# A pair's context parts in an attention kernel: turned by one transpose, scaled and added by VectorE

## The reference, cut to what matters

```python
q = (x @ Wq + bq).reshape(B, S, 16, 32).transpose(0, 2, 1, 3)      # B = 2, S = 2048
k = (x @ Wk + bk).reshape(B, S, 16, 32).transpose(0, 2, 1, 3)
v = (x @ Wv + bv).reshape(B, S, 16, 32).transpose(0, 2, 1, 3)
scores = einsum('bhqd,bhkd->bhqk', q / sqrt(32), k) + attention_bias
scores = where(mask, -inf, scores)
probs = softmax(scores, axis=-1)
ctx = einsum('bhqk,bhkd->bhqd', probs, v)
```

## Time and profile before

| | |
|---|---|
| median of 3 runs | 3609.03 us (3608.39 to 3610.77) |
| span of the profiled execution | 3605.5 us; the median of the runs is 3.5 us above it |
| TensorE busy, weight loads | 98%, 68% |
| VectorE, ScalarE, POOL busy | 59%, 61%, 61% over the span |
| DMA | 828.6 MB, 230 GB/s over the span, 337 GB/s from 550 to 2350 us |
| granted TensorE clock | 0.994 of full, 1.00 from 550 to 2350 us |

### The profile page before, as it was taken

The page is one execution under the profiler, slowest core; times in us unless marked ns, Lnnn a source line. Parts: engine busy times, 40 slices in busy tenths (PEclk is TensorE's granted clock), DMA queues, the critical chain, the costliest instruction groups (busy, mean ns, idle before and its releaser), DMA issues. The chain is left out here.

```text
span 3605.5 us, 79854 instructions
## 1 busy us (share of the span) xinstructions
PE 3541.5 (98%) x32051; PEld 2435.2 (68%) x32051; DVE 2119.2 (59%) x4375; ACT 2204.3 (61%) x3175; POOL 2186.5 (61%) x782
## 2 busy tenths in 40 slices
PE   7999999999999999999999999999999999999998
PEld 3444458888888888888888888887544444444444
DVE  7676668878788787878787887876211111111102
ACT  2343369999999999999999999997210211111110
POOL 1111169999999999999999999996310110110100
PEclk9999999999999999999999999999999999999998
DMA  5555598888998888998888988887310110111002
GB/s 195 199 187 193 187 386 324 323 334 324 349 379 323 326 324 329 389 341 327 327 324 335 383 334 327 331 326 262 120 35 0 35 35 19 40 47 44 15 24 94
DMA packets 210118, 828.62 MB, mean 230 GB/s; under 512 B 25044, under 2 KB 58964, under 8 KB 134488
## 3 DMA queue, kind: packets, MB, share of 16 engines
q1 hardware_dynamic: 204532, 815.09, 59.8%
q10 hardware_dynamic: 5220, 8.42, 0.6%
HBM read 732.19 MB, written 91.23 MB: 228 GB/s over the span
## 5 line engine op out<-in xcount | busy, mean ns | idle before, releaser
L1196 POOL TENSOR_TENSOR at_tiles<-at_tiles,at_negmask 128x1920 f32<-128x1920 f32 x509 | 1951.0, 3881 | 57.8 <-DMA at_tiles<-in_bias 46.5
L1297 ACT ACTIVATE at_tiles<-at_tiles,at_rmin 128x2048 f32<-128x2048 f32 x512 | 1030.3, 2012 | 2.4 <-DVE at_rmin L1357 2.4
L1236 PE MATMUL at_ps_p<-consts,at_tiles 128*128 128x128 f32 x8192 | 1024.9, 272 | 1.9 <-ACT at_prob_t L1307 1.5
L1307 ACT ACTIVATE at_prob_t<-at_ps_p 128x512 f32<-128x512 f32 x1664 | 898.4, 603 | 153.2 <-PE at_ps_p L1236 152.3
L1236 PEld LDWEIGHTS at_ps_p<-consts,at_tiles 128*128 128x128 f32 x8192 | 939.2, 142 | 71.8 <-ACT at_prob_t L1307 1.8
L1357 DVE CUSTOM_DVE_ANT_0 at_tiles<-at_ps_s,at_tiles,at_rmin 128x1024 f32<-128x1024 f32 x512 | 657.0, 1283 | 227.1 <-PE at_ps_s L1221 226.1
L1215 PE MATMUL at_ps_s<-at_k_stack,at_q_stack 128*128 128x512 f32 x2048 | 702.0, 439 | 8.1 <-DVE at_rmin L1357 6.1
L1357 DVE CUSTOM_DVE_ANT_0 at_tiles<-at_ps_s,at_tiles 128x1024 f32<-128x1024 f32 x512 | 624.3, 1219 | 24.1 <-POOL at_tiles L1196 22.0
L1255 PE MATMUL at_ps_c<-at_prob_t,at_v 128*32 128x128 f32 x16384 | 500.3, 274 | 0.9 <-ACT at_prob_t L1307 0.9
L1255 PEld LDWEIGHTS at_ps_c<-at_prob_t,at_v 128*32 128x32 f32 x16384 | 431.6, 110 | 43.7 <-issue 42.7
L1737 PE MATMUL ff_ps_m<-ff_w,ff_hid 128*128 128x512 f32 x1024 | 441.8, 593 | 0.0
(11 more groups left out here) (193 smaller groups left out, 2631.1 us busy)
## 6 DMA issues: line engine op xcount, KB each, us to landing
at_tiles<-in_bias SPq DMA_DIRECT2D x512, 1024.0 KB, 6.2
at_k_stack<-k_hi SPq DMA_DIRECT2D x128, 256.0 KB, 5.5
at_k_stack<-k_lo SPq DMA_DIRECT2D x128, 256.0 KB, 5.4
negm<-em_mask_out SPq DMA_DIRECT2D x32, 512.0 KB, 6.6
at_q_stack<-q_hi SPq DMA_DIRECT2D x128, 128.0 KB, 5.1
at_q_stack<-q_lo SPq DMA_DIRECT2D x128, 128.0 KB, 5.2
at_v<-v SPq DMA_DIRECT2D x64, 256.0 KB, 8.1
at_negmask<-negm SPq DMA_DIRECT2D x32, 512.0 KB, 9.6
```

The costliest lines, as they stand in the source:

```text
L1196: pool.tensor_tensor(tiles[s][:, 0:PCOLS], tiles[s][:, 0:PCOLS], negm[s][:, 0:PCOLS], ALU.add).then_inc(s_pool, 1)
L1236: last = pe.transpose(ps_p[k][:, y * P:(y + 1) * P], tiles[s][:, t * P:(t + 1) * P], ident)
L1297: act.activation(tiles[s][:, :], tiles[s][:, :], ACT.Exp, bias=rmin[:, s, 1:2], scale=-1.0, accum_out=rsum[:, s:s + 1]).then_inc(s_exp, 1)
L1307: act.activation(p_t[pr % 2][:, j, 4 * c:4 * c + 4, :].rearrange("p t q -> p (t q)"), ps_p[k][:], ACT.Copy).then_inc(s_pe[k], 1)
```

## The change

`parts_sum` becomes `parts_rows`: in place of the matmul with the stacked identities stands a transpose of `cx_sb` with the ordinary identity, 128x128, into columns 128 to 255 of the same bank. It turns the parts but doesn't add the halves. `context` on VectorE then has three operations in place of two: the reciprocal; a multiplication of all 128 columns by it, from PSUM back into `cx_sb`; and an addition of the two halves of `cx_sb`, from SBUF to SBUF, into `cx_all`. Each waits for the one before.

```diff
-            def parts_sum(pr):
+            def parts_rows(pr):
                 if not 0 <= pr < NP:
                     return
                 pe.wait_ge(s_cxs, pr + 1)
-                pe.matmul(ps_c[:, P:P + 2 * HD], cx_sb[:], stack, start=True, stop=True).then_inc(s_cxm, 1)
+                pe.transpose(ps_c[:, P:2 * P], cx_sb[:], ident).then_inc(s_cxm, 1)
@@ context, on VectorE
                 dve.wait_ge(s_cxm, pr + 1)
                 v.reciprocal(rinv[:], rsum[:, s:s + 2]).then_inc(s_rv, 1)
+                dve.wait_ge(s_rv, 2 * pr + 1)
+                v.tensor_tensor(cx_sb[:].rearrange("p (h j d) -> p h j d", h=2, j=2),
+                                ps_c[:, P:2 * P].rearrange("p (h j d) -> p h j d", h=2, j=2),
+                                rinv[:].unsqueeze(1).unsqueeze(3).broadcast_to([P, 2, 2, HD]), ALU.mult).then_inc(s_rv, 1)
                 after(dve, s_st[s // 2], 16 * (n // HEADS))
-                dve.wait_ge(s_rv, pr + 1)
+                dve.wait_ge(s_rv, 2 * pr + 2)
                 v.tensor_tensor(cx_all[:, s:s + 2, h * HD:(h + 1) * HD],
-                                ps_c[:, P:P + 2 * HD].rearrange("p (j d) -> p j d", j=2),
-                                rinv[:].unsqueeze(2).broadcast_to([P, 2, HD]), ALU.mult).then_inc(s_cxo, 1)
+                                cx_sb[:, 0:2 * HD].rearrange("p (j d) -> p j d", j=2),
+                                cx_sb[:, 2 * HD:].rearrange("p (j d) -> p j d", j=2), ALU.add).then_inc(s_cxo, 1)
```

More of the change, by code:

```diff
@@ L1201, in _ @@
             ident = net.consts[:, C_IDENT:C_IDENT + P]
-            stack = net.consts[:, C_STACK:C_STACK + 2 * HD]
             def qk(u, a):
@@ L1268, in _ @@
                 qk(u + 3, 1)
-                parts_sum(pr - 2)
+                parts_rows(pr - 2)
                 transposes(u, (2, 3))
@@ L1278, in _ @@
                 qk(u + 5, 1)
-                parts_sum(pr - 1)
+                parts_rows(pr - 1)
                 transposes(u + 2, (2, 3))
```

## The result

| | before | after |
|---|---|---|
| median of 20 runs each | 3609.82 us | 3631.80 us |
| lowest and highest | 3606.85 to 3611.40 | 3611.03 to 3672.47 |
| span of the profiled execution | 3605.5 us | 3635.5 us |

The ratio is 1.0053, with a 95% interval of 1.0037 to 1.0068: the change makes the kernel slower by half a per cent, as forecast (3639 us, range 3583 to 3725). The ratio is one of means and leaves out the three slowest executions of the changed kernel (3666 to 3672 us), so it is a little under the quotient of the two medians, 1.0061. A second thing stands in the table that the forecast did not name: executions of the kernel before agree within 5 us, those of the changed one are spread over 61 us.

What follows compares the result with a forecast made beforehand. TensorE was taken to bound the kernel. Its -31 us was outweighed by held additions: short-lead heads -6, other heads +28, slips +12, together +34, taken as +30 on 3609: 3639 us, own range 3618 to 3675, stated range 3583 to 3725.

Steps and rivals of the forecast that it cites:

- TensorE's saving: Attention stage: a transpose for the stacked matmul saves TensorE 0.12 us a pair, -31 us over 256 pairs.
- the rival without a lock: Late transfers make each addition's wait random, 0 to 3.82 us: 3861 us; chance 0.18 together with many slips.
- The hold: In `context`, the addition with two SBUF inputs stands until POOL's operation ends, up to 3.82 us.
- The lock, the drift and the slip: Additions end with POOL's operations; waits shrink 0.12 us a pair, then one misses: held 3.82 us, TensorE loses 2.9.
- The room: After the second context of a turn, the addition may be 0.9 us late before TensorE stands still.
- The sum: Short-lead heads -6 us, 52 other heads +28, four slips +12: together +34, taken as +30, so 3639 us.
- the long lock: Additions locked to POOL's ends with POOL at least 4.95 us ahead: heads of 32.0 us, +0.54 on today.
- the middle lock: Later name for the prediction's "long lock", forecast at 32.0 us a head for 52 heads, +28 us.
- The lead that was called not to be had: POOL's time ahead of VectorE on a turn's second tile: 4.95 us wanted, 4.4 today, 3.9 with shorter heads.
- The half-way rival of "many slips": Many misses of POOL's ends, between forecast and no lock: some 3720 us; chance 0.18 together with no lock.
- Full gain: Rival: additions held under 0.9 us on average or only briefly, TensorE's saving arrives: 3583 us; chance 0.29 including most of it.
- the short lock: Additions end with POOL's operations, lead 1.1 to 2.0 us: heads of 30.98 us, -0.48; expected in 12 heads.

Runs made afterwards that it cites:

- the first experiment: Changed kernel with the addition as two operations, each reading one half from PSUM and one from SBUF: 3579.2 us, ratio to before 0.9919.
- the second: Kernel before with its stacked matmul, product sent to the buffer, plus a VectorE maximum with both inputs from SBUF: 3654.2 us, ratio 1.0123.
- The slower POOL: Changed kernel with POOL masking 1952 columns of a tile in place of 1920, TensorE the other 96: 3591.8 us, ratio 0.9951.

## Why the prediction was right

**TensorE's saving: right.** A transpose saves what was said: heads that nothing delays take 31.01 us, against 31.47, which is 0.115 us a pair (0.12 in the prediction), and the first experiment brings 30.3 us of the 31.

**VectorE's arithmetic: right.** The product takes 291 ns (292), the free addition 225 (225).

**Two readings that were wrong and changed nothing.** TensorE's waits for VectorE before are not "1.5 us in all": that is one row, and all of them make 5.4 us. VectorE's 226.1 us for the scores are one row too; it waited 131.5 us more for the context parts. In the rival without a lock, 256 times the loss is 286 us and not 283.

**The hold: right, by three operations of another stage.** The trace of before had no such case in the attention stage; three in the next stage were enough. Three experiments show it from three sides: take one SBUF input away and it goes (the first), put it into the old kernel and it comes (the second), cut POOL's operation to 240 columns and it goes. The Trainium skill's rule ("SBUF — State Buffer", "Who interferes with whom": a VectorE instruction with two SBUF inputs contends with a GpSimd instruction that reads SBUF; one with at most one SBUF input does not, outside its two-port modes) is borne out in both halves by the operations of `context`. The rule's exception for those modes is missing in the prediction and in the expectation of the first experiment, and the trace of before has a case that may be one: line 1919 reads one tensor from SBUF, with scalars by the row.

```profile
L1919 DVE TENSOR_SCALAR ff_norm<-ff_res,ff_mv,ff_rstd x32: 514/518/1484, 2530.6 to 3373.9; 128x512 f32<-128x512 f32 x32
```

The one of 1484 ns is the operation at 2538.71, begun 0.07 us after POOL's run of four; the prediction read it only for what it cost POOL. In which mode it ran no run here shows. Nor does every operation of POOL hold one of two SBUF inputs: in the embedding stage a subtraction and multiplication of 128x512 with two (line 754) takes 742 to 753 ns in all 32 cases, though many run beside a POOL operation on 128x4 of 1457 ns. That POOL hardly pays is right too: 3875 ns an operation before and after.

**The lock, the drift and the slip: right.** The additions of heads 1 to 3 shorten from 1.2 to 0.3 us, the next takes 3.84. The head with the slip lasts 2.9 us more. The room was under-sized a little: at the second context records of 1.39 us, 1.17 over the free 0.225, stand in a head that lasts 31.02 us, so it is about 1.2 us, not 0.9. The slower POOL shows the lock without the drift.

**The sum: right in its total, wrong in two terms that made up for each other.** The profiled execution is 30 us over the one before, the +30 of the forecast. But 4.3 us of them lie ahead of the attention stage, where the change touches nothing: its first transpose starts at 496.8 us in place of 492.5, and the granted clock over the first 250 us is 0.95, against 0.97. The stage itself is 25.6 us longer. Against TensorE's own pace of 31.01 us, 63 heads carry 59.8 us too much; the kernel before carries 5.2 over its 31.47, and the saving is 63 x 0.46 = 29 us:

| | heads | us over own pace |
|---|---|---|
| start of the stage | 0 | 5.0 |
| single slips and the third mask reload | 4, 35, 47 | 9.1 |
| way into the longest lock, and in and about it | 19 to 26 | 29.5 |
| all others | 51 | 16.2 |

The failed step is "the long lock wants 4.95, so the head lasts 1.0 us longer: 32.0 us". In the middle lock a head lasts 31.4 us (mean of 42, without head 47): a little less than before, not 0.54 more. The lead that was called not to be had is there: second tiles have 4.35 to 5.2 us. The larger room is one reason, as the lead then need only be 5.85 - 1.2 = 4.65. Two more stand in the records of tile 81, which is waited for by POOL in a head of 31.07 us and has a lead of 4.60: its transfer took 7.25 us, where tile 193 took 7.65 before, and from VectorE's first use to the first transpose it is 10.11 us, against 10.28. Together that is 0.9 of the roughly 1.0 us; what made the transfers quicker was not tried. So the forecast's +28 us for 52 such heads is some -5 us for 42 (together 14.7 us over 31.01 a head, where before they would be 19). What filled its place is a state that the forecast left out: two misses close together, and a lead of 8.2 us at 34.9 us a head, 29.5 us in all. The half-way rival of "many slips" has more of that in it than the forecast has, and with a spread of 61 us it is luck that the total came out.

**The rivals.** Full gain is what the first experiment gives, 3579 us for 3583, by removing the hold, not in the changed kernel. Its remark that equal beats would never leave the short lock is what the slower POOL shows. No lock at all (3861 us) did not occur: the slowest of the 73 executions of kernels with a held addition and POOL near its full length took 3678 us.

## What to carry to other kernels

Count the SBUF inputs of every VectorE operation that runs beside a busy POOL. Here two made it wait for the end of POOL's additions of 128x1920, 225 ns becoming up to 3.95 us; one of them read from PSUM made the same step free, and faster than both kernels at 3579 us. Where a short operation is held by the end of a long periodic one, look at the ratio of the two beats and not at the mean hold: the same hold of about 1 us cost at most 13 us, POOL's own slower pace included, where POOL was slightly the slower engine, and 39 to 53 us where it was slightly the faster (over the 3579.2 us of the first experiment).

## What was not expected

- A kernel got 40 us faster by giving its second-busiest engine more work (3591.8 us with 1952 columns, medians of 3617.8 and 3631.8 with 1920).
- The hold turned a kernel whose executions agree within 5 us into one that varies by 61 us. The granted clock reads 1.00 from 550 to 2350 us in both, but in the changed kernel that mean hides 3.4 us at half in head 19, just where the longest lock begins.
- Once in the lock with a lead of 8.2 us, it stays for one to four heads, each up to 3.6 us longer than before. In the five traces that met it (changed kernel three times, the one with `pv` waiting for the product, old kernel with the added operation) it began with two long holds close together.
